# A state-space mixer takes its B products to TensorE, and its units become 4 states by 256 tokens

## The reference, cut to what matters

```python
h = layernorm(x, ln_g, ln_b)
xs, gate = split(h @ in_w, 2)
xs = silu(conv4(xs) + conv_b)
Bm, Cm = split(xs @ xp_w, 2)
dt = softplus(Bm @ dt_w + dt_b)
A = -exp(A_log)
hst = hst * exp(dt[..., None] * A) + dt[..., None] * Bm[:, None, :] * xs[..., None]   # over t
y = sum(hst * Cm[:, None, :], -1)
y = (y + D_skip * xs) * silu(gate)
return y @ out_w + res
```

## Time and profile before

| | |
|---|---|
| median of 3 executions | 5252.27 us (5251.64 to 5253.35) |
| span of the profiled execution, first to last instruction | 4960.9 us |
| own time of the profiled execution | not given apart from its span |
| median less span | 291.4 us |
| mean granted clock of TensorE | 0.904 |
| layer-2 mixer, first convolution matmul to last output | 1746.8 to 2653.5 us of the span |

### The profile page before, as it was taken

How to read it: one execution, slowest core, us unless ns; L and a number is a source line. 1 busy time by engine, 2 the same in 40 slices (tenths; PEclk the granted TensorE clock), 3 DMA queues, 4 the chain that set the end, 5 groups by cost and what they waited for, 6 DMA issues and landing times. The chain is left out here.

```text
span 4960.9 us, 46627 instructions
## 1 busy us (share of the span) xinstructions
PE 3814.6 (77%) x13222; PEld 1745.4 (35%) x13222; DVE 3629.3 (73%) x5288; ACT 2514.6 (51%) x3881; POOL 2956.4 (60%) x2245
## 2 busy tenths in 40 slices
PE   5444565999649978888787799998978777777776
PEld 2111223754226633333333454553423222222222
DVE  7999774134547679999998544545543899999998
ACT  4444431344538856666664344444355555555554
POOL 4888465027254479999993211114420798889987
PEclk7777788999869999999999898989989999899998
DMA  1110211112211144444441432321100444444342
GB/s 50 43 43 9 84 38 55 68 57 76 97 56 58 43 143 156 154 154 157 156 152 62 89 43 38 42 34 48 61 9 34 142 134 141 134 138 140 129 141 98
DMA packets 161698, 434.77 MB, mean 88 GB/s; under 512 B 28150, under 2 KB 51384, under 8 KB 160048
## 3 DMA queue, kind: packets, MB, share of 16 engines
q1 hardware_dynamic: 142512, 374.41, 24.7%
q0 software_dynamic: 18944, 57.57, 3.3%
HBM read 363.67 MB, written 68.68 MB: 87 GB/s over the span
## 5 line engine op out<-in xcount | busy, mean ns | idle before, releaser
L1673 ACT ACTIVATE mb_h<-m_dt,m_a_neg 128x512 f32<-128x512 f32 x1024 | 665.0, 681 | 724.0 <-DVE r L1828 332.8
L1532 PE MATMUL mb_y<-r,m_diag_y 128*128 128x512 f32 x1024 | 546.9, 669 | 275.8 <-POOL r L1753 164.8
L1819 DVE TENSOR_TENSOR_SCAN mb_h<-mb_h,m_u 128x1024 f32<-128x1024 f32 x320 | 734.0, 2294 | 10.4
L1776 POOL TENSOR_TENSOR m_u<-m_bsb,m_xs 128x1024 f32<-128x1024 f32 x256 | 599.9, 2366 | 175.7 <-DMA m_bsb<-bc_rows 175.7
L1776 POOL TENSOR_TENSOR m_u<-m_bsb,m_dtx 128x1024 f32<-128x1024 f32 x256 | 596.2, 2358 | 49.1 <-DVE m_dtx L1860 27.9
L1532 PE MATMUL mb_y<-m_hc,w_common 128*128 128x512 f32 x1024 | 495.3, 623 | 153.3 <-DVE m_hc L1828 87.2
L1819 DVE TENSOR_TENSOR_SCAN m_hs<-mb_h,m_u 128x1024 f32<-128x1024 f32 x192 | 437.5, 2279 | 1.7 <-POOL m_u L1776 1.7
L1532 PEld LDWEIGHTS mb_y<-r,m_diag_y 128*128 128x128 f32 x1024 | 196.1, 207 | 622.2 <-POOL r L1753 244.0
L2302 DVE TENSOR_REDUCE at_mx<-at_ps_s 128x4 f32<-128x512 f32 (+1 forms) x256 | 242.8, 957 | 233.6 <-PE at_ps_s L2116 233.6
L1753 POOL TENSOR_TENSOR r<-m_hs,m_csb 128x1024 f32<-128x1024 f32 x128 | 306.0, 2391 | 119.1 <-DVE m_hs L1819 118.5
L1532 PEld LDWEIGHTS mb_y<-m_hc,w_common 128*128 128x128 f32 x1024 | 190.4, 196 | 450.5 <-issue 191.6
(11 more groups left out here) (518 smaller groups left out, 8519.4 us busy)
## 6 DMA issues: line engine op xcount, KB each, us to landing
m_bsb<-bc_rows SPq DMA_DIRECT2D x256, 512.0 KB, 4.9
m_csb<-bc_rows SPq DMA_DIRECT2D x256, 512.0 KB, 4.0
at_q<-q_parts SPq DMA_DIRECT2D x144, 128.0 KB
x_slots<-d_zeros SPq DMA_DIRECT2D x8, 1024.0 KB, 5.0
kept_x<-r SPq DMA_DIRECT2D x2, 4096.0 KB, 14.1
xg_xg<-x_slots SPq DMA_DIRECT2D x32, 256.0 KB, 2.6
y_slots<-xg_yo POOLq DMA_DIRECT2D x32, 256.0 KB, 2.3
xl_xg<-x_slots SPq DMA_DIRECT2D x32, 256.0 KB, 2.6
```

The lines of the kernel that those rows point to most:

```text
L1532: mm = nc.tensor.matmul(ps_y[:, h], weight, hc[:, q % RING, s], start=False, stop=g == GROUPS - 1 and s == SG - 1)
L1673: ins = nc.scalar.activation(ps_h[:, q % 2, s], dt[:, i % 2, h], ACT.Exp, scale=a_neg[:, n:n + 1])
L1776: nc.gpsimd.tensor_tensor(u[:, q % RING], bsb[:, n % RING], dtx[:, i % 2, h].unsqueeze(1).broadcast_to([P, SG, TILE]), ALU.mult).then_inc( ...
L1819: V.tensor_tensor_scan(flat(to), flat(ps_h[:, q % 2]), flat(u[:, q % RING]), 0.0, ALU.mult, ALU.add).then_inc(h_ready, 1)
```

## The change

A new function `scan_mixer` takes the place of `mamba` in layer 2; layer 3 keeps `mamba`. In it:

- A unit is 4 states (SN) of one half of the channels over the 256 tokens of one sequence. It has 1024 elements as before, and there are 16 to a tile again. Two successive units (the two sequences) share a "super" v, for which ACT computes four decays of 512.
- TensorE makes u. dt x is transposed to have tokens on the partitions (`turn_z`, then a copy to `zt`), and so is B (`turn_b`, `bt`). GpSimd spreads B on a diagonal: `dg[token, token', state]` is B at token = token', and zero elsewhere, for blocks of 64 tokens (`spots` is a unit matrix of 64, twice). A matmul of zt by dg over 64 rows gives u for 64 tokens and 4 states, 256 columns. Four of them, on rows 0 to 63 and 64 to 127 in turn, make a unit (`make_u`), written to the two banks of `ps_u[:, q % 2]`.
- DVE scans each state on its own, 256 elements with a step of four in PSUM, so no decay has to be zeroed. The C product is GpSimd's for five units of six, and DVE's for the sixth.
- The decays go to SBUF (`dec`, three supers), the B broadcasts are gone, and C comes as 4 states a transfer into two buffers.

```diff
+        by_pool = [q % 6 != 5 for q in range(NU)]
...
+            def make_u(q):
+                i, g, h, s = place(q)
+                d = (i * SGROUPS + g) * 2 + s
+                if q % SUBS == 0:
+                    pe.wait_ge(z_ready, 2 * i + 2)
+                pe.wait_ge(d_ready, d + 1)
+                if q >= 2:
+                    taken(q - 2, pe)
+                for kk in range(2):
+                    for j in range(2):
+                        at = slice(j * QT, (j + 1) * QT)
+                        mm = nc.tensor.matmul(ps_u[:, q % 2, j].rearrange("p (t k n) -> p k t n", k=2, n=SN)[:, kk], zt[at, i % 2, h, s * 2 + kk],
+                                              dg[at, d % DR, kk], start=True, stop=True)
+                mm.then_inc(u_made, 1)
+
+            def sum_states(v):
+                i, g, h, _s = place(2 * v)
+                if v % SUPERS == 0:
+                    if i:
+                        pe.wait_ge(yg_ready, 2 * i)
+                    for k in range(2):
+                        nc.tensor.matmul(ps_y[:, k], diag_d[:, k], xs[:, i % 2, k], start=True, stop=False)
+                products(2 * v + 2, pe)
+                for n in range(SN):
+                    mm = nc.tensor.matmul(ps_y[:, h], w["eye"], hc[:, v % HCR, n], start=False, stop=g == SGROUPS - 1 and n == SN - 1)
+                mm.then_inc(y_used, 1)
...
+            for q in range(NU + 6):
+                i, n = q // SUBS, q % SUBS
+                if q < NU:
+                    make_u(q)
+                if q % 2 == 0 and q >= 6:
+                    sum_states(q // 2 - 3)
+                if q >= NU:
+                    continue
+                a = i + 1
+                if n in (0, 1) and a < NT:
+                    conv(a, n)
+                if n in (2, 3):
+                    gate(i, n - 2)
+                if n == 5 and a < NT:
+                    project_bc(a)
+                if n == 6 and a < NT:
+                    turn_b(a)
+                    step_size(a, 0)
+                if n == 7 and a < NT:
+                    step_size(a, 1)
+                if n == 9 and i:
+                    project_out(i - 1)
+                if n in (12, 13) and a < NT:
+                    turn_z(a, n - 12)
...
+            for v in range(NS):
+                i, n = v // SUPERS, v % SUPERS
+                decay(v)
+                if i + 1 < NT:
+                    ahead(i + 1, n)
+                if n == 1:
+                    silu_gate(i, 0)
+                    silu_gate(i, 1)
+                    exp_table(2 * i)
...
+            def diagonals(d):
+
+                i, g, s = d // (2 * SGROUPS), d // 2 % SGROUPS, d % 2
+                pool.wait_ge(bt_ready, i + 1)
+                if d >= DR:
+                    pool.wait_ge(u_made, (d - DR) // 2 * 4 + 2 + s + 1)
+                G.tensor_tensor(dg[:, d % DR], w["spots"].unsqueeze(1).unsqueeze(3).broadcast_to([P, 2, QT, SN]),
+                                bt[:, i % 2, 2 * s:2 * s + 2, g * SN:(g + 1) * SN].unsqueeze(2).broadcast_to([P, 2, QT, SN]),
+                                ALU.mult).then_inc(d_ready, 1)
...
+            def scan(q):
+                i, g, h, s = place(q)
+                v = q // 2
+                dve.wait_ge(da_ready, v + 1)
+                dve.wait_ge(u_made, q + 1)
+                if by_pool[q] and pool_units[q] >= HSR:
+                    dve.wait_ge(hp_ready, pool_units[q] - HSR + 1)
+                at = slice(s * T, (s + 1) * T)
+                flat = ps_u[:, q % 2].rearrange("p j c -> p (j c)").rearrange("p (t n) -> p n t", n=SN)
+                for n in range(SN):
+                    to = hs[:, pool_units[q] % HSR, n] if by_pool[q] else flat[:, n]
+                    ins = V.tensor_tensor_scan(to, dec[:, v % DECR, n, at], flat[:, n], 0.0, ALU.mult, ALU.add)
+                ins.then_inc(h_ready, 1)
...
+            for q in range(NU):
+                i, n = q // SUBS, q % SUBS
+                scan(q)
+                if not by_pool[q]:
+                    times_c(q)
+                if n == 5 and i:
+                    gated(i - 1)
+                if n == 11 and i:
+                    finish(i - 1)
...
-        mamba(nc, w, parts, False, r0, xn, xn, bc_d)
+        scan_mixer(nc, w, parts, r0, xn, xn, bc_d)
```

More of the change, by code:

```diff
@@ L3378, in groups_of @@
     mamba3, once3 = mamba_pieces(np, a, "L3_attn", True)
-    mamba2.update({"ln1_g": col(a["L2_attn_ln1_g"]), "ln1_b": col(a["L2_attn_ln1_b"])})
+    mamba2.update({"ln1_g": col(a["L2_attn_ln1_g"]), "ln1_b": col(a["L2_attn_ln1_b"]),
+                   "spots": np.tile(np.eye(QT, dtype=np.float32), (2, 1))})
     experts1 = expert_pieces(a["L1_ffn_w1"], a["L1_ffn_w2"])
```

271 lines of the change are left out of this document (added).

## The result

| | before | after |
|---|---|---|
| median of four executions | 5251.95 us (5238.73 to 5253.35) | 5456.85 us (5446.13 to 5459.86) |
| ratio, 95% interval | | 1.039 (1.0367 to 1.0413) |
| own time / span of the profiled execution | not given / 4960.9 us | 5459.86 / 5458.2 us |
| mixer, first convolution matmul to last output | 906.7 us | 1977.0 to 3096.9, 1119.9 us |

The change costs 205 us where 168 were forecast; 5456.85 lies in the range of 5330 to 5520. The mixer grew by 213.2 us, by the forecast it should have reached 1074.9, so it is 45 us longer than that.

A forecast was written before the change was run, and what follows sets the result against it. TensorE was to become the mixer's bound: 1014 us of work, a 43.5 us wait for yg, plus start and end, make the mixer 168 us longer; 5252 + 168 = 5420 us, range 5330 to 5520.

The forecast's parts named there:

- the prediction's terms: TensorE's mixer work: 686 us kept, 219 for u, 17.5 for transposes, 464 row changes at 0.197; together 1014.
- TensorE becomes the bound: In the layer-2 mixer, TensorE's tile takes 63.4 us, above DVE's 45.6 and today's 54.7.
- faster: Rival: DVE and GpSimd pace the mixer at 45.7 us a tile, TensorE's tile being under 54.7; 5110 us, chance 0.04.
- u side by side, 0.857 a unit: TensorE's u matmuls on the two halves of 64 rows overlap: 13.7 us a tile, against 27.4 in a line.
- The pair of the earlier trace: Evidence for overlap: two xl_spread matmuls on rows 0 to 31 and 64 to 95 took 1.06 us, not 1.71.
- Changes of rows, 0.197 each: TensorE pays this when its matmuls switch row ranges: 29 changes a tile instead of 2, 5.7 us a tile.
- Wait for yg: TensorE's skip matmuls wait for DVE's gating of the tile before: 2.9 us on average in 15 tiles, 43.5 us.
- DVE and GpSimd: Their mixer work per tile was priced at 45.6 us for DVE and 45.7 for GpSimd, under TensorE's 63.4.
- The start: Mixer's beginning: the first u starts about 1771.3, after 8 transposes and two copies that follow dt x.
- lost overlap: Two row groups lose the share that four do by the skill's 3.07: u 286 us, not 219; time 5487.
- cheaper seams: Rival: row changes hide behind waits and the yg wait is short; 5377 or 5285 us, chance 0.18.

The follow-up runs named there:

- e1: Changed kernel with both u matmuls of a pair on rows 0 to 63, so they cannot run side by side; 5397.32 us, ratio 1.0865.
- e2: Changed kernel with u of two units made in one burst, so that rows change less often; 5185.25 us, ratio 1.0455.
- e3: Changed kernel with the gate's silu on ACT one super later; 5140.85 us, ratio 1.0368.
- e4: Changed kernel with the gate's silu one super later and DVE's gating after unit 4, not 5; 5125.72 us, ratio 1.0322.
- e5: Changed kernel with the products of two of each four states left out of TensorE's sum; 5057.23 us, ratio 1.0191.
- e6: Changed kernel with dt x and the diagonals rounded to bf16 for the u matmuls; 5085.43 us, ratio 1.0262.
- e7: Changed kernel with half of the C products on DVE, instead of one in six; 5215.46 us, ratio 1.0512.
- e8: Changed kernel with the edits of e2 and e4 together: bursts of two units, gate later, gating earlier; 5094.3 us, ratio 1.027.
- e9: The kernel of e8 with the u matmuls in bf16 as well; 5012.85 us, ratio 1.0107.
- e10: Changed kernel with the C products and the unit matrix of the sums in bf16, u in fp32; 5033.43 us, ratio 1.014.
- e11: Changed kernel with the edits of e10, e6 and e4: sums and u in bf16, gate and gating moved; 4882.43 us, ratio 0.9835.

## Why the prediction was right, and what it missed

The whole set can be put on one line per kernel. TensorE's own work at full clock, by the prediction's terms, against what a trace gives for it: the mixer less TensorE's idle time in it, times the mean granted clock.

| kernel | mixer | idle | clock | (mixer - idle) x clock | by the terms |
|---|---|---|---|---|---|
| changed | 1119.9 | 55.2 | 0.96 | 1022 | 1014 |
| e1, same rows | 1336.7 | 22.7 | 0.94 | 1236 | 1014 + 219 = 1233 |
| e2, pairs | 1117.0 | 87.5 | 0.97 | 997 | 982 (165 changes fewer in the trace) |
| e3, gate later | 1090.4 | 37.1 | 0.97 | 1021 | 1014 |
| e4, and gating | 1059.8 | 16.9 | 0.98 | 1020 | 1014 |
| e5, half the sums | 1001.8 | 138.6 | 0.94 | 813 | 1014 - 219 = 795 |
| e6, u bf16 | 1034.8 | 131.5 | 0.93 | 841 | 1014 - 165 = 849 |
| e7, C on DVE | 1154.1 | 71.0 | 0.95 | 1024 | 1014 |
| e8, pairs, gate, gating | 1040.0 | 38.4 | 0.99 | 992 | 982 |
| e9, and u bf16 | 957.5 | 96.0 | 0.95 | 821 | 982 - 165 = 817 |
| e10, sums bf16 | 968.0 | 191.1 | 0.89 | 688 | 685 |
| e11, both bf16 | 826.7 | 220.3 | 0.82 | 498 | 1014 - 329 - 165 = 520 |

The work agrees with its terms within 2.3%, but for e11 with 4%, and that one stays open: its low clock falls on busy and idle time alike, so the mean is not to blame. What is left of each mixer is idle time and clock. They mostly grow together, but e1 has little idle time and a clock of 0.94.

- **TensorE becomes the bound: right.** It is idle for 5% of the mixer, and doubling its u, 219 us by the terms, added 218 us to the time (e1), if with the help of two changes that cancelled. The rival "faster" needed a tile under 54.7 us; it came at 68.0 (from skip to skip, 2027.78 in tile 1 to 3047.1 in tile 16).
- **u side by side, 0.857 a unit: right**, by single records and by e1. The pair of the earlier trace rows, 32 rows each, was a fair guide to four pairs of 64 rows in succession. The 3.07 of the Trainium skill (TensorE: Matmul & The Clock Gate, "Measured speedup vs the span model"), which stands there for four groups, has no counterpart in these two.
- **Changes of rows, 0.197 each: right in sum.** With 464 of them the work comes to 1014; the traces have 455, and give 1020 to 1024 for the kernels with as many. The drain of which the Trainium skill (TensorEngine Tiling, "Key Properties") speaks agrees with that. e2 and e8 have 165 fewer and 25 to 30 us less work by the table, so the ones that went were 0.15 to 0.18 us each.
- **Wait for yg: right in its chain, a little large.** 34.7 us against 43.5, in 15 tiles. (The forecast's own times, 12.35 against 10.0 and 1.14 more in one tile of three, make 2.7 a tile and 41 us, not 2.9 and 43.5.) e3 takes one link out and leaves 20.3; e4 takes both and leaves none.
- **DVE and GpSimd: right, and cheaper than priced.** A scan of 256 paces at 0.583 us (forecast 0.635), a diagonal takes 1.04 (forecast 1.25), the C product 2.355 as before. They were 45.6 and 45.7 us a tile by the sum and are 42.3 and 44.5 by these.
- **The start:** first u 26.6 us after the first convolution matmul, where 24.5 were forecast.
- **The term that was missing: the clock.** The forecast has 1014 us of work and 60.9 of idle time; the trace has 55.2 of idle time, and 1064.7 that is not idle. Stretches at half clock add up to 89 us of the mixer and so take 45 out of it, 39 of them where TensorE has work. With these 39, 11.6 more of work than the terms have, and 5.7 less of idle time, the error of 45 is complete. Some 10 of the 45 fall in the first 60 us, where the kernel before lost 8. I read the 0.97 of the earlier trace rows as "TensorE works at 2.4 GHz", and did not ask what 0.03 or 0.04 is worth on an engine that has become the bound, nor what the new waits would do to it. e4 shows the link: with the wait gone, idle time and lost clock fell together.

The step that failed is thus the claim that the sum of TensorE's work at full clock and its waits is the length; the missing term is a third one, 39 us, and it hid in the margin of the range, which was made for other things (lost overlap, cheaper seams). Forecast +168, measured +213 in the mixer.

What brings the clock down is not settled. It is not waiting alone. In the changed kernel 13 of the 15 falls past the start come behind the wait for yg, six within 1.4 us of its end and seven 8 to 11 us after it; but in e4 all six past the start come without a wait, and in e1 twelve of seventeen do. Nor is it the work of 16 rows alone: e8 has all of that and more idle time than e4, and its clock stayed at 1.00 for 980 us. What e8 has fewer of is changes of rows, but so has e2, which falls again to 0.97, with 70 us of short waits on scans. No run changed the 16-row work by itself.

## What to carry to other kernels

When work moves to an engine that had slack, price what that slack was hiding: not only its waits but its clock, which cost nothing before and costs its full share after. Work taken off an engine that waits for the next one to free its buffers comes back in good part as waiting: 219 us off the sums gave 118, 165 off u gave 85. (That more than two buffers of u would help is likely by these waits, but no run had them.) So first move what the tile waits for as a whole (here the gating), then shorten the work; in that order the same cut was worth more (nothing that can be told for the pairs alone, 20 us after the gating was moved).

## What the runs showed of the hardware

- fp32 matmuls are the price here: the same sum of 512 columns is two records of 0.4286 us in fp32 and one in bf16, where sums in succession start 0.215 us apart (e10; its work is 688 us, 685 by that).
- GpSimd's product took 2.355 us whether its output was fp32 or bf16, and its diagonals 1.04 us with either; both operands of a diagonal are broadcast views, and that is less than the 1.27 of the same number of elements in a plain addition.
- For the changed kernel the two kinds of chip differ by 271 us outside the mixer, 229 of them ahead of it, and by 4 us in it.
